# First frequency scratch laid out frequency, quarter, row, column, with one load in place of four

## The reference

```
h  = relu(bn(layernorm(t) @ w1.T))            # 96 -> 192 columns
X  = fft(h, axis=tokens, norm='ortho')
xr = relu(X.real*rd - X.imag*idg + rb)
xi = relu(X.imag*rd + X.real*idg + ib)
y  = ifft(xr + 1j*xi).real
t  = t + bn(y @ w2.T)                         # 192 -> 96 columns
```

## Time and profile before

| | before |
|---|---|
| median of 3 runs | 5097.38 us |
| the runs | 5085.65, 5097.38, 5097.47 us |
| profiled execution, its own time | 5094.76 us |
| its span | 5092.8 us |
| TensorE busy (matmuls) | 4692.9 us, 92% of the span |
| VectorE, ScalarE, GpSimd busy | 3398.0, 3389.3, 2513.4 us |
| DMA, all queues | 1072.01 MB, 210 GB/s on average |
| granted TensorE clock, mean | 0.972 |

### The profile page before, as it was taken

How to read it: one execution, slowest core, us unless ns; L and a number is a source line. 1 busy time by engine, 2 the same in 40 slices (tenths; PEclk the granted TensorE clock), 3 DMA queues, 4 the chain that set the end, 5 groups by cost and what they waited for, 6 DMA issues and landing times.

```text
span 5092.8 us, 151731 instructions
## 1 busy us (share of the span) xinstructions
PE 4692.9 (92%) x62292; PEld 3120.1 (61%) x62292; DVE 3398.0 (67%) x6475; ACT 3389.3 (67%) x5511; POOL 2513.4 (49%) x1508
## 2 busy tenths in 40 slices
PE   8989999999999989999948999999999999999986
PEld 8955555555555544444436666666666666666663
DVE  1156776677677865777715767777777776777676
ACT  4455665656566558888736777777777777777763
POOL 0067777777777755666613433343334334333431
PEclk9999999999999999999959999999999999999997
DMA  7657767776777779999947777777777767777762
GB/s 163 158 146 182 193 179 181 184 194 178 188 189 185 179 202 414 416 418 414 380 130 185 202 192 198 193 194 199 197 200 186 204 189 192 200 199 198 184 171 62
DMA packets 499822, 1072.01 MB, mean 210 GB/s; under 512 B 176608, under 2 KB 324608, under 8 KB 466240
## 3 DMA queue, kind: packets, MB, share of 16 engines
q1 hardware_dynamic: 499136, 1062.31, 72.5%
HBM read 557.40 MB, written 484.44 MB: 205 GB/s over the span
## 4 chain that ended last, share of the span: by engine, by line
PE 32%; DMA 8%; DVE 5%; issue 2%; ACT 1%; SPq 1%; POOL 1%; DVEq 0%; POOLq 0%; ACTq 0%
PE bank_w_s L1474 6%; PE bank_o L1452 4%; PE bank_x L1421 4%; DMA bt<-a_scratch 3%; PE bank_w_s L1485 3%; PE bank_c L1440 2%; PE bank_c L1433 2%; PE bank_c L1430 2%; DMA a_scratch<-a 2%; PE bank_l L1400 2%; PE bank_l L1342 2%; DMA tb<-t_scratch 1%; PE bank_x L1418 1%; PE bank_l L1358 1%; PE bank_l L1371 1%
## 5 line engine op out<-in xcount | busy, mean ns | idle before, releaser
L772 POOL TENSOR_TENSOR hlo<-h,hhi 128x1682 f16<-128x1682 f32 x288 | 977.6, 3394 | 377.8 <-DVE hhi L825 377.8
L735 ACT ACTIVATE h<-c1ps,s 128x1568 f32<-128x1568 f32 x288 | 479.3, 1664 | 625.4 <-PE c1ps L651 625.4
L785 DVE BATCH_NORM_STATS2 stats<-z 128x6 f32<-128x392 f32 x1152 | 597.1, 560 | 436.6 <-ACT z L725 426.4
L683 PE MATMUL dwps<-hhi,taps 64*64 64x392 f16 x13824 | 691.2, 330 | 12.6 <-issue 12.6
L683 PE MATMUL dwps<-hlo,taps 64*64 64x392 f16 x13824 | 683.6, 328 | 6.0 <-issue 6.0
L1668 POOL TENSOR_TENSOR s_plus<-d_minus,imag_scaled 128x448 f32<-128x448 f32 (+1 forms) x192 | 213.5, 1112 | 708.9 <-ACT imag_scaled L1535 708.9
L930 ACT ACTIVATE z2m<-z2m,s 128x784 f32<-128x784 f32 x512 | 489.6, 1029 | 105.2 <-DMA z2m<-z_scratch 104.8
L1677 POOL TENSOR_TENSOR onat<-tb,o 96x448 f32<-96x448 f32 x224 | 236.4, 1062 | 620.8 <-DVE o L1737 620.8
L954 POOL TENSOR_TENSOR h_split<-z2m,h_split 128x1568 f16<-128x1568 f32 x128 | 405.3, 3166 | 266.6 <-DVE h_split L993 266.6
L683 PEld LDWEIGHTS dwps<-hhi,taps 64*64 64x64 f16 x13824 | 380.6, 106 | 253.3 <-issue 107.0
L683 PEld LDWEIGHTS dwps<-hlo,taps 64*64 64x64 f16 x13824 | 405.0, 106 | 187.3 <-issue 8.4
(11 more groups left out here) (234 smaller groups left out, 9673.0 us busy)
## 6 DMA issues: line engine op xcount, KB each, us to landing
z_scratch<-z SPq DMA_DIRECT2D x1152, 196.0 KB, 3.3
z2m<-z_scratch SPq DMA_DIRECT2D x64, 1960.0 KB, 15.8
z2m<-z_scratch SPq DMA_DIRECT2D x64, 1568.0 KB, 11.5
a_scratch<-a SPq DMA_DIRECT2D x224, 384.0 KB, 3.9
bt<-a_scratch SPq DMA_DIRECT2D x384, 168.0 KB
t_scratch<-y SPq DMA_DIRECT2D x32, 1344.0 KB, 8.9
c_scratch<-cc SPq DMA_DIRECT2D x128, 336.0 KB, 3.8
d<-c_scratch SPq DMA_DIRECT2D x128, 336.0 KB, 4.7
```

The costliest lines, as they stand in the source:

```text
L683: ins = nc.tensor.matmul(dw[64 * j:64 * j + 64, r, g, 0:QN], taps[half, u, da, dx, :, :].rearrange("p y c -> p (y c)"), part[half, s, a0:a ...
L735: nc.scalar.activation(to, src, ACT.Relu, bias=s1[:, 1, u:u + 1], scale=s1[:, 0, u:u + 1]).then_inc(h_ready, 1)
L772: nc.gpsimd.tensor_tensor(to, h, hi, ALU.subtract).then_inc(lo_ready, 1)
L785: nc.vector.bn_stats(stats[:, i, v, at:at + 6], z2[:, v % 3, g, r, :]).then_inc(s_stat, 1)
```

## The change

The scratch tensor `a_scratch` gets the order image, frequency (32), quarter (4), class, column, in place of image, row 32q + k, class, column. Its size is the same. `store_a` writes the same 128 rows of 3 KB from the same tile; on the DRAM side the access is now quarter (4), frequency (32), 768 floats. `load_b` reads the same rows of 768 bytes to the same places with one transfer for all four quarters, because quarter and class now lie next to each other in DRAM and merge into one dimension of 112. The semaphore counts of `ld_b` follow.

```
-    a_d = nc.dram_tensor("a_scratch", (NB, 128, NJ, H), F32, kind="Internal").ap()
+    a_d = nc.dram_tensor("a_scratch", (NB, 32, 4, NJ, H), F32, kind="Internal").ap()
...
-        for q in range(4):
-            src = a_d[f, 32 * q + k0:32 * q + k0 + n].rearrange("k j c -> j k c")
-            sp.dma_start(bt[NJ * q:NJ * q + NJ, k0:k0 + n, :], src).then_inc(ld_b[k], 16)
+        src = a_d[f, k0:k0 + n].rearrange("k q j c -> (q j) k c")
+        sp.dma_start(bt[:, k0:k0 + n, :], src).then_inc(ld_b[k], 16)
...
-        sp.dma_start(a_d[f, :, 4 * p:4 * p + 4, :].rearrange("p j c -> p (j c)"), v).then_inc(st_a[p], 16)
+        to = a_d[f, :, :, 4 * p:4 * p + 4, :].rearrange("k q j c -> q k (j c)")
+        sp.dma_start(to, v).then_inc(st_a[p], 16)
...
-                pe.wait_ge(ld_b[k], m * 64 + 64)
+                pe.wait_ge(ld_b[k], m * 16 + 16)
-            pe.wait_ge(ld_b[k0 // 8], m * 64 + 64)
+            pe.wait_ge(ld_b[k0 // 8], m * 16 + 16)
```

## The result

| | before | after |
|---|---|---|
| median | 5097.43 us (4 runs) | 5586.13 us (4 runs, 5580.59 to 5588.89) |
| span of the profiled execution | 5092.8 us | 5586.9 us |
| TensorE busy | 4692.9 us | 4926.9 us |
| granted clock, mean | 0.972 | 0.919 |

The ratio is 1.0946, with a 95% interval of 1.0924 to 1.0968: slower by 489 us, 15.3 us for each image. The forecast was 5280, with a range up to 5410. The direction was right, the size far too small.

A forecast was written before the change was run, and what follows sets the result against it. The prediction took a per-image loop through the last store of `a` and the load of `bt`, without slack, as the bound. Store +7.1, load -0.4, caught up -1.0 gave +5.7 us, times 32 +182: 5280 us, range 5165 to 5410.

The forecast's parts named there:

- The narrow cut: Store of `a`: its DRAM-side outer dimension of 4 puts it on 4 DMA engines in place of 16.
- the walk: Last five stores of an image followed through the DMA queue: last one lands 7.9 us later, 7.1 taken.
- rival 1: Store of `a`: queue drains better, only the bare 3.0 us are seen, +83 us, 5180 us; chance 0.15.
- The load: Load of `bt`: 16 engines in place of 14 gain 0.4 us an image; saved SP issue time counted as nothing.
- what is late next: Behind the last store: SP waits at L1257, TensorE at the first spectrum group; 1 us an image taken back.
- The sum: Per image: +7.1 store, -0.4 load, -1.0 caught up, so +5.7 us; times 32, +182 us.
- The buffers of `a` hold: Copies into `a`: the last store's issue slips by about 1 us, which costs nothing.
- I take 1 us back: TensorE's idle time: VectorE and ScalarE catch up in the pause, 1 us an image, bounds 0 and 3.
- the price of a row: Store of `a` alone: 126 ns of an engine a row, so 32 rows on an engine are 4.0 us.
- Rival 2: Four engines become the bound, two more chain DMA legs each meet a 4.0 us store: +438, 5535 us; chance 0.15.
- rival 3: Store of `a` keeps its 16 engines, only the load's gain of 13 to 54 us is left: about 5070; chance 0.08.
- rival 4: Store on four engines, but nothing seen, as the loop has slack the chain doesn't show; chance 0.02.

The follow-up runs named there:

- e1: Changed kernel with each store of `a` made as four transfers of 32 rows, one for each quarter: 5090.13 us.
- e2: Kernel before, old order and four loads, with the scratch padded to 33 rows a quarter so the store's DRAM-side outer dimension is 4: 5608.05 us.
- e9: Changed kernel with stores 0 to 5 each made as four transfers of 32 rows, only the last store on 4 engines: 5369.20 us.
- The filler: 24 small-table matmuls, results overwritten, before each image's first spectrum group: 5504.67 us in the changed kernel, 5292.15 us in e9.
- e7: Changed kernel with four buffers for `a` in place of two: 5526.35 us.
- e10: Changed kernel with stores 0 to 5 on 4 engines and only the last made as four transfers of 32 rows: 5407.16 us.
- e14: Kernel before, scratch padded, each store made as four transfers of 4 x 8 rows, on 4 engines reading partitions 8 apart: 5466.32 us.
- e8: Kernel before with the scratch padded to 65 rows for 64, so the store's DRAM-side outer dimension is 2: 6164.75 us.
- e11: Kernel before, scratch padded to 33 rows for 32, each store two transfers of 64 rows, on two engines reading partitions 32 apart: 6220.85 us.
- e4_four_loads: Changed kernel with each load made as four transfers for the four quarters again: 5601.60 us.

## Why the prediction was wrong

**Right.** The narrow cut: the store leaves 4 completions, and without it nothing is lost (e1, e2). No row of before could decide this for two sides of different size (128 and 4). The rule in the Trainium skill, "DMA: Bandwidth & Descriptors", section "Why a DMA increments its semaphore by 16 and not by 1", named 4; the trace after agrees, with 4 completions. The path through the last store is the right one too: in e9 its cut alone costs 279 us.

**Right in the number only.** The last store's landing: 7.9 us later by the walk, 7.1 taken, and the leg is 6.2 to 7.0 longer (8.8 to 9.4 against 2.4 to 2.6). But the walk had it wait in the queue behind the other narrow stores. In e9 there are none, and the leg is still 8.7 us. And the bare price, 3.0 us in rival 1, is over 6 there. Two errors met in a right number. The load: 0.4 us an image by its 16 engines, about 0.5 measured and not clear of noise. In the chains it is the issues, counted as nothing, that are gone, and the transfer is not shorter.

**The step that failed: what is late next.** The sum stops at the landing. It takes TensorE's wait by its length and then 1.0 us off. Per image, TensorE's time in the two profiled executions splits without a rest: it is idle 260.1 us more (8.1) and busy 234.0 us more for the same work (7.3), together 15.4. The wait for the load alone, 5.3, comes near the 5.7 of the sum; the rest was not in it. Three terms were wrong.

1. *The clock, left out altogether.* TensorE comes out of a wait at a granted clock of 0.51 to 0.64, and the 7.3 us of slower matmuls are the largest term. The filler takes back 81 and 77 us in two kernels, 2.4 to 2.5 us an image for the one wait that it covers; the other waits' share is argued from busy times (e7, e10), not tested with a filler.
2. *"The buffers of `a` hold".* ScalarE waits 136.0 us for them, and TensorE waits 103.5 us for ScalarE behind it, 3.0 an image more than before. With the last store wide (e10) the six other narrow ones lose 317 us, 202 of them in the clock, and this overlaps with the loss behind the last store by 100.
3. *"I take 1 us back".* Of the 260.1 us of idle time the wait for the load has 169.1 (204.6 less 35.5, 5.3 an image) and the wait behind the buffer 96.1 (103.5 less 7.4). That is 5 us too much over 32 images, so by this account 0.2 us an image were caught up, not 1.0.

**Also wrong, but not what decides: the price of a row.** "Alone, a row of the store costs ... 126 ns ... 32 rows are 4.0" took the price from a store on 16 engines; here it is 180 ns in the mean, and the lone store lands 8.7 us after its issue, not 5.3. With 133 ns (e14) the buffers still don't hold (ScalarE waits 91.5 us), and the loss is still 363 us. By this run some 120 of the 306 us that the forecast missed are the price, and more if its issues cost something.

**The rivals.** Rival 2 came nearest with 5535, but its arithmetic, two more legs of 4.0 us on the chain, is not what happened: the chain after shows two long store legs and a slow clock. Whether its premise holds, that the four engines are the bound, is open. The DMA share of 0.59 over that image of 92.2 us can't tell, being a mean over 16 engines. An estimate from it and the 180 ns: 0.59 x 92.2 x 16 = 870 us of engine time, of which the seven stores have 7 x 128 x 0.18 = 161, so 44 us are left for each engine, and 7 x 32 x 0.18 = 40 more for each of the four. That is some 84 of 92 us, nearly full. Full engines are not needed for the larger part of the loss (e9 has one narrow store of seven and loses 279 us); for the rest nothing separates them from the buffers. Rivals 1, 3 and 4 fell: the loss is far over 83 us, the store has 4 completions, and the loop has no slack.

## What to carry to other kernels

When an access pattern is rearranged, look at the outermost dimension of both sides of every transfer that touches the tensor, not only of the one that is to be saved: a small one there (4 where there were 128 rows) moves the same bytes over fewer DMA engines. Price a narrow transfer from a narrow one, and look whether its first rows cost what its last ones do. Then ask of each buffer that the transfer frees who waits for it. And a new wait of the busiest engine costs more than its length if the granted clock is lower behind it: read the clock by stretch, and count the work of the low stretch at up to twice its time (the first spectrum group took 3.76 us in place of 2.04).

## What the runs showed of the hardware

- A 3 KB row of a store alone, in ns of one DMA engine, as a mean over the store: 126 on 16 engines and 221 on 16 engines with two rows of a transfer each (e1_four_stores); 205 on 8; 180 on 4, and 133 on 4 with blocks of 8 rows (e14); 121 on 2 (e8, e11). Another row step in DRAM changed nothing (173 and 178). The forecast had the same price at any number.
- On 4 engines the rows of the lone store took 274 ns over its first 2 us and 126 over its last 3.5.
- After waits of TensorE of 3.3 us (for a buffer) and 6.9 us (for the load), the granted clock was 0.64 and 0.51 over the next 8 us. In an image of the kernel before it was 1.00.
- Four buffers in place of two made TensorE's waits 58 us longer and the kernel 60 us shorter, as its matmuls took 122 us less (e7).
- Twelve issues fewer an image on SyncE, 5.1 us of its time, and a load on 16 engines in place of 14 gained together some 15 us, 0.5 an image, which is inside the interval of the comparison (e4_four_loads against the changed kernel).
